# Mixture-of-experts layer on one core: gelu rows turned by DMA and VectorE instead of TensorE, second products three tiles behind the first

## The reference

```python
x  = x + ((x * ys) @ W0) * d                       # first layer, per batch modulation
shared = silu(x @ w1) * (x @ w3) @ w2
s = sigmoid(concat(x, t_emb) @ router_W); top-2 of s + router_bias; gates normalised
h = gelu(x @ W1e[e]);  y = h @ W2e[e]              # for each expert e
out = x + (shared + sum_e combine[:, e] * y_e) / 3
```

## Time and profile before

| | |
|---|---|
| time of three runs | 1102.67 us median, 1099.77 to 1103.0 |
| profiled execution, device time | 1101.17 us |
| its span in the trace | 1099.4 us, so 1.8 us lie outside it |
| TensorE busy | 1065.8 us, 97% |
| VectorE, ScalarE, GpSimd busy | 480.8, 315.1, 337.2 us |
| packets of ScalarE's DMA queue (q10) | 36,992, 17.83 MB |
| stage three on TensorE | from 652 us to the end |

### The profile page before, as it was taken

One profiled execution on the slowest core, in us unless ns is written; L12 is line 12 of the kernel. 1 busy time (PEld: TensorE's weight loads), 2 busy tenths in 40 slices (PEclk: granted clock), 3 DMA queues, 4 the chain that ended last, 5 costly groups with the idle time before them and its releaser, 6 DMA issues.

```text
span 1099.4 us, 15779 instructions
## 1 busy us (share of the span) xinstructions
PE 1065.8 (97%) x4976; PEld 870.7 (79%) x4977; DVE 480.8 (44%) x767; ACT 315.1 (29%) x488; POOL 337.2 (31%) x316
## 2 busy tenths in 40 slices
PE   7999999999999999999999989999999999999996
PEld 6767778788888888888888868888878888888885
DVE  5556537568323333333232134444444444444442
ACT  4332333232222222221111122333333333333331
POOL 0000000001134334333304002366545554555454
PEclk9999999999999999999999999999999999999998
DMA  4556587768778675877616439966568888875544
GB/s 174 192 191 196 206 283 237 271 250 252 281 250 272 217 271 207 261 251 253 222 38 204 66 118 296 292 100 99 98 119 189 181 187 195 185 156 87 85 77 48
DMA packets 131789, 207.76 MB, mean 189 GB/s; under 512 B 25312, under 2 KB 97888, under 8 KB 122528
## 3 DMA queue, kind: packets, MB, share of 16 engines
q1 hardware_dynamic: 59744, 143.27, 39.6%
q0 software_dynamic: 35024, 46.28, 21.5%
q10 hardware_dynamic: 36992, 17.83, 6.9%
HBM read 111.01 MB, written 96.54 MB: 189 GB/s over the span
## 4 chain that ended last, share of the span: by engine, by line
PE 86%; DMA 6%; DVE 4%; SPq 1%; ACT 1%; issue 1%; POOLq 0%; POOL 0%; ACTq 0%; DVEq 0%
PE banks L503 13%; PE banks L505 12%; PE banks L504 12%; PE banks L439 9%; PE banks L440 9%; PE banks L441 9%; PE banks L453 4%; PE banks L454 4%; PE banks L455 4%; PE banks L496 3%; DMA we_d<-ehl 3%; PE banks L405 2%; PE banks L407 2%; PE banks L406 2%; DMA xin<-xT 1%; DMA eraw<-expert_w 1%
## 5 line engine op out<-in xcount | busy, mean ns | idle before, releaser
L1134 POOL DMA_INDIRECT out<-ys,row x142 | 223.0, 1570 | 262.9 <-DVE ys L1043 157.0
L439 PE MATMUL banks<-xh,w13h 128*128 128x512 f32 x512 | 200.1, 391 | 1.9 <-DVE w13l L746 1.9
L440 PE MATMUL banks<-xl,w13h 128*128 128x512 f32 x512 | 199.9, 390 | 0.0
L441 PE MATMUL banks<-xh,w13l 128*128 128x512 f32 x512 | 199.8, 390 | 0.0
L768 DVE SCALAR_TENSOR_TENSOR gm<-sil,banks 128x512 f32<-128x512 f32 x64 | 43.9, 686 | 244.0 <-ACT sil L596 244.0
L503 PE MATMUL banks<-we,xgth 128*128 x284 | 118.8, 418 | 5.7 <-issue 5.4
L596 ACT ACTIVATE sil<-banks 128x512 f32<-128x512 f32 x64 | 38.2, 597 | 292.2 <-PE banks L441 292.2
L439 PEld LDWEIGHTS banks<-xh,w13h 128*128 128x128 f32 x512 | 96.5, 189 | 22.4 <-DVE w13l L746 2.2
L503 PE MATMUL banks<-we,hidth 128*128 x284 | 112.4, 396 | 1.8 <-issue 1.7
L1030 DVE TENSOR_TENSOR xgtl<-xgt,xgth 128x512 fp32r<-128x512 f32 x71 | 49.2, 692 | 147.6 <-ACT xgth L653 147.6
L441 PEld LDWEIGHTS banks<-xh,w13l 128*128 128x128 f32 x512 | 96.5, 189 | 20.2
(11 more groups left out here) (156 smaller groups left out, 1478.4 us busy)
## 6 DMA issues: line engine op xcount, KB each, us to landing
we_d<-ehl SPq DMA_DIRECT2D x32, 1024.0 KB, 6.3
xg<-xs_d ACTq DMA_DIRECT2D x136, 128.0 KB, 4.0
eraw<-expert_w SPq DMA_DIRECT2D x32, 512.0 KB, 5.2
we<-we_d SPq DMA_DIRECT2D x8, 2048.0 KB, 8.7
we<-we_d SPq DMA_DIRECT2D x32, 512.0 KB, 4.4
xin<-xT SPq DMA_DIRECT2D x8, 1024.0 KB, 6.5
x1t_d<-x1t SPq DMA_DIRECT2D x8, 1024.0 KB, 8.6
xin<-x1t_d SPq DMA_DIRECT2D x8, 1024.0 KB, 9.0
```

Source lines behind the costliest of these rows:

```text
L439: pe.matmul(ps[hc % 2][:, :], w_hi, xh[:, j, c, :], start=(c == 0), stop=False)
L440: pe.matmul(ps[hc % 2][:, :], w_hi, xl[:, j, c, :], start=False, stop=False)
L441: last = pe.matmul(ps[hc % 2][:, :], w_lo, xh[:, j, c, :], start=False, stop=(c == DC - 1))
L1134: pool.indirect_dma_start(out_half, IO(row2[:, h, t:t + 1], 0), ys[:, t % RING, h * D // 2:(h + 1) * D // 2], None, compute_op=ALU.add).th ...
```

## The change

TensorE no longer transposes. ScalarE's gelu writes `hid` with its channel groups reordered, four DMAs on ScalarE's queue (`move_h`) copy it within the chip's memory into `hturn` in 512-byte runs, and VectorE's 32 x 32 transposes (`turn_h`) complete the turn into `hidt`, which the two splits then read in place of PSUM. `hid` and `hturn` become rings of four tiles. TensorE does matmul1(t) and then matmul2(t-3). All loops of stage three are written out on TensorE, ScalarE and VectorE. The lookup of a tile's expert is done once, in the middle of the first product before it, instead of ahead of both products. The next rows (`load_pair`) are asked for at another place in ScalarE's order. A tile's rows are now taken so that a partition quarter j and row r hold slot 4r + j, hence the new `xs_rec`.

```diff
-        hid = sb("hid", [2, HE], FP32, 128)
+        hid = sb("hid", [RING, HE], FP32, 184)
+        hturn = sb("hturn", [RING, SUB, P], FP32, 160)
+        hidt = sb("hidt", [2, DC, P], FP32, 140)
...
-            sp.dma_start(slot[:, :, :], xs_rec).then_inc(slots_in, 16)
+            for j in range(SUB):
+                sp.dma_start(slot[j * Q:(j + 1) * Q], xs_rec[j]).then_inc(slots_in, 16)
...
-            def transpose_h(t, k):
-                pe.wait_ge(hid_done, t + 1 + 2)
-                pe.wait_ge(hidt_done, t + 1)
...
                 for c in range(DC):
-                    last = pe.transpose(ht_ps[k % 2][:, c * P:(c + 1) * P], hid[:, k % 2, c * P:(c + 1) * P], ident)
-                last.then_inc(th_done, 1)
...
-            with pe.Fori(0, TURNS) as i:
-                for k in range(1, RING + 1):
-                    t = RING * i + k
-                    matmul1(t, k)
-                    matmul2(t - 1, k - 1)
-                    transpose_h(t, k)
...
+            for t in range(TILES + LAG):
+                if t < TILES:
+                    matmul1(t)
+                if t == LAG:
+                    pe.wait_ge(o_done, SUB * NBLK)
+                if t >= LAG:
+                    matmul2(t - LAG)
...
+            def hidden(t):
...
                 act.wait_ge(mm1_done, t + 1)
...
+                if t >= RING:
+                    act.wait_ge(hturn_done, t - RING + 1)
+                act.activation(hid[:, t % RING, :].rearrange("p (g c n) -> p c g n", g=SUB, n=Q),
+                               h_ps[t % 2][:, :].rearrange("p (c g n) -> p c g n", g=SUB, n=Q), ACT.Gelu).then_inc(hid_done, 1)
+
+            def move_h(t):
+
+                act.wait_ge(hid_done, t + 1 + 2)
+                for g in range(P // Q):
+                    act.dma_start(hturn[g * Q:(g + 1) * Q, t % RING], hid[:, t % RING, g * P:(g + 1) * P]).then_inc(h_moved[t % RING], 16)
+
+            def h_high_of(t):
+
+                act.wait_ge(hturn_done, t + 1)
+                if t >= 2:
+                    act.wait_ge(mm2_done, t - 2 + 1 + 1)
+                act.activation(hidth[:, t % 2], hidt[:, t % 2], ACT.Copy).then_inc(hidth_done, 1)
+
+            x_high_of(0)
+            load_pair(2)
+            for t in range(TILES + TURN_LAG):
+                if t + 1 < TILES:
+                    if t:
+                        act.wait_ge(mm1_done, t)
+                    x_high_of(t + 1)
+                if t < TILES:
+                    hidden(t)
+                    if t == 0:
+                        act.wait_ge(o_done, SUB * NBLK)
+                    move_h(t)
+                if t >= TURN_LAG:
+                    h_high_of(t - TURN_LAG)
+                if t % 2:
+                    load_pair((t + 1) // 2 + 2)
...
+            def turn_h(t):
+
+                dve.wait_ge(h_moved[t % RING], 16 * (P // Q) * (t // RING + 1))
+                if t >= 2:
+                    dve.wait_ge(hidt_done, t - 2 + 1 + 2)
+                dve.transpose(hidt[:, t % 2].rearrange("p c (a r) -> p a c r", r=Q),
+                              hturn[:, t % RING].rearrange("p a (c n) -> p a c n", n=Q)).then_inc(hturn_done, 1)
...
+            for t in range(TILES + LAG + 1):
...
+                if t > LAG:
+                    take_y(t - LAG - 1)
                 if t + 1 < TILES:
...
+                    take_x(t + 1)
+                if t + 2 < TILES:
+                    turn_x(t + 2)
+                if 0 <= t - TURN_LAG < TILES:
+                    turn_h(t - TURN_LAG)
+                    take_h(t - TURN_LAG)
```

More of the change, by code:

```diff
@@ L33 @@
 SLOTS = PADDED * P
-TURNS = TILES // RING
+TURN_LAG = 2
+LAG = TURN_LAG + 1
 PADROWS = P
@@ L164, in shared_moe_kernel @@
         rank_ps = bank[0]
-        ht_ps, h_ps, y_ps = bank[0:2], bank[2:4], bank[6:8]
+        h_ps, y_ps = bank[2:4], bank[6:8]
         x1t_d = nc.dram_tensor("x1t_d", [NBLK, P, DC, BLK], FP32)
@@ L490, in _, with product @@
                     shared_block(2 * h + j, j)
-            def transpose_h(t, k):
-                pe.wait_ge(hid_done, t + 1 + 2)
-                pe.wait_ge(hidt_done, t + 1)
+            def product(ps, high, low, place, m, midway):
                 for c in range(DC):
-                    last = pe.transpose(ht_ps[k % 2][:, c * P:(c + 1) * P], hid[:, k % 2, c * P:(c + 1) * P], ident)
-                last.then_inc(th_done, 1)
-            def product(ps, high, low, place, m):
-                for c in range(DC):
+                    if c == 2:
+                        midway()
                     w_hi, w_lo = (we[:, bass.ds(place, 1), m, c // 2, part, c % 2, :].rearrange("p a n -> p (a n)") for part in range(2))
@@ L517, in matmul1, with matmul2 @@
                 pe.wait_ge(hid_done, t + 1)
-                product(h_ps[k % 2][:, :], xgth[:, k % 2], xgtl[:, k % 2], place, 0).then_inc(mm1_done, 1)
-            def matmul2(t, k):
-                turn, place = expert_of(t)
+                product(h_ps[t % 2][:, :], xgth[:, t % 2], xgtl[:, t % 2], place, 0, lambda: look_up(t + 1)).then_inc(mm1_done, 1)
+            def matmul2(t):
+                turn, place = expert_of[t]
                 pe.wait_ge(weights_in, 2 * turn + 2)
@@ L655, in experts_step @@
-            def experts_step(t, k, turn, more=True, rows=True):
+                act.activation(xgth[:, t % 2], xgt[:, t % 2], ACT.Copy).then_inc(xgth_done, 1)
+            def hidden(t):
                 act.wait_ge(mm1_done, t + 1)
-                act.activation(hid[:, k % 2, :], h_ps[k % 2][:, :], ACT.Gelu).then_inc(hid_done, 1)
-                if more:
-                    take_x(t + 1, k + 1)
-                    if k % PAIR == 0 and rows:
-                        act.wait_ge(xturn_done, t + 2)
-                        load_rows(t + RING, k, turn + 1)
-                act.wait_ge(th_done, t + 1)
-                act.activation(hidth[:, k % 2].rearrange("p c n -> p (c n)"), ht_ps[k % 2][:, :], ACT.Copy).then_inc(hidth_done, 1)
@@ L1073, in _ @@
-            take_y(TILES - 1, TILES - 1)
+                dve.tensor_scalar(ys[:, t % RING, :], y_ps[t % 2][:, :], slot[:, t, 1:2].bitcast(FP32), None, ALU.mult).then_inc(ys_done, 1)
+            turn_x(0)
+            turn_x(1)
+            take_x(0)
+            output(NBLK - 1)
+            for t in range(TILES + LAG + 1):
+                if t == 1:
+                    dve.wait_ge(slots_in, 16 * SUB)
+                    for h in range(2):
+                        dve.tensor_scalar(row2[:, h, :], slot[:, :, 0], 2.0, float(h), ALU.mult, ALU.add).then_inc(halved, 1)
+                if t > LAG:
+                    take_y(t - LAG - 1)
+                if t + 1 < TILES:
+                    take_x(t + 1)
[4 more added lines that the diff above has]
+                    take_h(t - TURN_LAG)
```

101 lines of the change are left out of this document (33 added, 68 removed).

## The result

| | before | after |
|---|---|---|
| median of the comparison's 20 runs each | 1101.94 us (1096.77 to 1107.67) | 1094.67 us (1089.74 to 1103.35) |
| ratio, 95% interval | | 0.9944 [0.9925, 0.9963] |
| profiled execution, its span | 1101.17, 1099.4 us | 1098.22, 1096.4 us |

What follows compares the result with a forecast made beforehand. TensorE (busy 97%) bounds the kernel now, the scatter chain afterwards: first scatter 673.2, tile 5 719.5, tile 70 1060.5, plus 7.25 and 1.8 us, gives 1070 us. Its own range is 1063 to 1082, 8 in 10 from 1055 to 1098.

Steps and rivals of the forecast that it cites:

- Work leaves TensorE, 48 us: Stage three on TensorE: dropped transposes save 35.5 us over 71 tiles (5.94 to 5.44 us each), written-out loops 12.6 us.
- The seams: TensorE at each loop round's end: 17 gaps of 0.74 us, 12.6 us, vanish if the jump causes them.
- The lookups: Expert lookups in mid-product on TensorE: cost nothing, or up to 0.3 us a tile if its queue runs dry.
- It fits with 1.2 us to spare: ScalarE's passes, issues and waiting for a pair of tiles: 9.7 us against TensorE's 10.9 us.
- Rival 2: ScalarE's issues or late moves set the pace, 5.7 to 5.9 us a tile; 1084 us, up to 1100; chance 0.16.
- Scatters set the end: GpSimd's scatter chain, not TensorE's, ends the kernel 9 us later, so the 48 us gain shrinks to about 31.
- quiet 4.95 us: Scatter time per tile on GpSimd away from weight transfers: 4.71 us before, 4.95 us with the added moves.
- the 0.24 us for the moves: Scatters in quiet stretches: the added moves cost 0.24 us more per tile, bounds nothing and 0.83 us.
- 0.26 to 0.5 us a tile for turns taken by packets: DMA engines alternate between queue rows packet by packet, so scatter packets wait for move packets, 0.26 us a half.
- Beside pieces 5.7 us: Scatter time per tile beside the 32 weight pieces: capacity taken as 5.45 us, 5.7 us with the moves.
- Start of the stage: Start of stage three: first second product at 669.0 to 671.7, `ys` at 671.9, first scatter at 673.2, 4.6 us later.
- Gelu's reordered write unchanged: ScalarE's gelu writing reordered channel groups: duration taken as unchanged, with bounds of nothing and 0.3 us.

Runs made afterwards that it cites:

- a_nr_sp: The changed kernel without the 32 weight pieces of 512 KB and with the moves issued on SyncE's queue instead of ScalarE's; 1079.6 us.
- b_unroll: The kernel before the change with its three loops of stage three written out, nothing else changed; 1093.89 us, 0.993 of the kernel before.
- bu_moves_late: The written-out kernel before, plus four unused moves of each tile's gelu rows, issued behind the high half of h on ScalarE; 1100.49 us.
- bu_moves: The written-out kernel before, plus four moves of each tile's gelu rows into an unread buffer, issued right behind the gelu on ScalarE; 1244.78 us.
- a_pair: The changed kernel with the moves of two tiles in one set of four issues and second products four tiles behind; 1107.08 us.
- a_half: The changed kernel with only the first half of each scatter, so half of each row is not added to the output; 1085.97 us.
- a_nr_sp_half: The changed kernel without the 32 weight pieces, with moves issued on SyncE's queue and only the first half of each scatter; 1071.44 us.
- a_pair1k: The changed kernel with two tiles' moves in one set and their rows side by side, giving 1024-byte runs; 1104.48 us.

## Why the prediction was right or wrong

- *Work leaves TensorE, 48 us*: right in kind, 3 us too large. 29.3 us of busy time went, and a_nr_sp shows the 5.44 us. The seams go with the loops (b_unroll), but they were 9.4 us and not 17 x 0.74 = 12.6: I took one round's step for all of them. The Trainium skill says that a taken jump out of the current pages stalls the fetch (Runtime: NRT & Kernel Launch, Instruction fetch mechanics); that the seams vanish in straight code agrees. The lookups cost nothing where TensorE is fed (a_nr_sp). In the change itself eight places from tile 10 on show a step of 0.42 to 0.85 us at them, where 0.23 is usual.
- *"It fits with 1.2 us to spare"*: wrong. I priced the moves' issues by those of row loads, 0.46 us each. They take 0.62 us, and those of row loads went from a median of 346 to 514 ns. The pair needs some 10.8 us of its 10.88 and not 9.7. Rival 2, with its 0.57 us an issue and 5.7 us a tile, described this closely, though its own sum of 11.4 us adds up passes and issues that partly run side by side. I had given it 0.16 as an alternative; it was true beside the forecast's own limit. Measured as limits, the two are 6.28 us beside pieces (scatters) and 5.65 to 5.8 us everywhere (ScalarE).
- *Scatters set the end*: right, as place. The quiet 4.95 us was measured as 5.02 and 4.83, with the 0.24 us for the moves. The prediction's 0.26 to 0.5 us a tile for turns taken by packets is near this in quiet stretches, where 4.71 became 5.02; beside the weight transfers it gives too little, 9.3 us became 11.8 at the start. It is no test of the page, though. In the Trainium skill (DMA: Bandwidth & Descriptors, Queues, rings and completion order) a packet is a group of typically 9 to 17 descriptors. I had put the profile's packets, single runs of 512 bytes, in its place.
- *"Beside pieces 5.7 us"*: wrong, and the step that failed: the price of a scatter beside the weight pieces, a term that was sized too small, is the largest miss, 16.8 of 28.1 us. I had 6.26 us from the rows and took 0.81 off it, because GpSimd waited for VectorE at times. Then I added the moves' quiet price. Neither stands: 6.28 us was measured, and the added moves cost 0.3 to 0.4 us where the engines are already shared (b_unroll 6.03 to 6.15 and bu_moves_late 6.34 to 6.55, with the same work on TensorE). That b_unroll, without any moves, has 6.1 us where TensorE asks for 5.94 shows that the 6.26 us read from the rows was nearly the capacity itself.
- *Start of the stage*: too early by 4.9 us. The first second product starts at 671.69, inside my count of 669.0 to 671.7; but I had taken its early end. It ends near 674.4, and some 1.7 us of that are the lower clock between 667.25 and 670.99. `ys` comes only at 676.55 (timeline, the kernel after):

```profile
672.52 2.71 ACTq L666 DMA_DIRECT2D hturn<-hid  x4
...
675.27 0.63 ACT L673 ACTIVATE hidth<-hidt 128x512 fp32r<-128x512 f32 x1 [2.78 <-issue]
...
675.94 0.69 DVE L1063 TENSOR_TENSOR hidtl<-hidt,hidth 128x512 fp32r<-128x512 f32 x1 [3.25 <-ACT hidth L673]
...
676.55 0.74 DVE L1071 TENSOR_SCALAR ys<-banks,slot 128x512 f32<-128x512 f32 x1
```

  `ys` stands in VectorE's queue behind the low half, which waits for the high half, which stands on ScalarE behind four issues. Then the first three periods are 11.8 to 12.0 us (10.3 on average up to tile 5), where I had kept 9.3, the price before any moves: I applied the moves' surcharge to every stretch but this one.
- *Gelu's reordered write unchanged*: right, 0.58 to 0.60 us, as in bu_moves.

Why removing one limit gives so little: the change has two of nearly one size. Without pieces 1083.25, half scatters 1085.97, without pieces and with the issues off ScalarE 1079.6, all three 1071.44 us.

Left open: why a move's issue takes 0.6 us and a row load's 0.35 to 0.5; why executions of one kernel differ by up to 13.6 us, so that a_pair's profile lies 3.8 us below its median and the change's 3.6 us above; and what sets a scatter's price beside the weight pieces. It goes with how full the 16 DMA engines are (78% before, 93% after), but no run varied that alone.

## What to carry to other kernels

An issue of a DMA is work of the engine that makes it, with a price of its own for each shape of transfer: price a new one by bounds from both sides, and if the upper bound fills the engine, the engine is a limit. Where the bounding engine's tile is cut from 6.08 to 5.44 us, list all that needs more than 5.44: here it was two things, and removing either alone moved the end little. Try the plain part of a change by itself: writing the loops out gave all of the gain, with none of the DMA traffic. And do not multiply one seam by the number of rounds: add up the steps of the whole trace.

## What the runs showed of the hardware

- An issue takes 0.35 to 0.51 us for a row transfer and 0.60 to 0.62 us for a move (medians over a kernel; 603 ns on SyncE in a_nr_sp). ScalarE starts no pass meanwhile, but a pass begun just before runs on beside the issues (890.85 and 890.88 us above). For the kernel after, by line (min, median, max of one in ns, first and last start):

```profile
L666 ACTq DMA_DIRECT2D hturn<-hid x284: 554/623/2037, 654.4 to 1069.3; - x142
...
L646 ACTq DMA_DIRECT2D xg<-xs_d x136: 309/514/1628, 649.2 to 1043.7; - x136
```

- ScalarE loaded its gelu table in every loop round, 17 x 1.28 us; with the loop written out, once. It hid behind TensorE in both.
- Beside 2 MB transfers q10 went from 17.3% to 45.1% of the 16 engines' time with 2.2 times the packets, and a scatter's period from 9.3 to 11.8 us (the first three tiles).
- Half a scatter beside them takes as long as a whole one (9.7 and 10.2 us a tile over tiles 0 to 5 in a_half and a_nr_sp_half, 10.3 and 10.0 in the change and a_nr_sp).
- Behind 5.03 us of idling TensorE's granted clock was 0.50 (727.90 to 732.00 us, the kernel after), with matmuls 0.43 us apart instead of 0.23; the same spacing stands behind waits of 3.92 us (667.25) and 5.22 us (725.17 in a_nr_sp_half).
- A period of scatters beside 512 KB pieces is hardly sensitive to the other queue's run length (a_pair 6.19 to 6.47 us at 512 bytes, a_pair1k 6.05 to 6.30 us at 1024, while the packets of q10 fell from 75,648 to 57,728).
